# Moving half of a forward transform behind the transform of the convolution's kernel

## What is computed

```python
K = 2 * real(einsum('hn,hnl->hl', Ct, exp(dtA * l)))          # the convolution's kernel, per channel
Xf = rfft(x, n=2 * length); Kf = rfft(K, n=2 * length)
y = irfft(Xf * Kf)[:, :length]                                  # a long causal convolution
r = x + y + x * D
x = x0 + layernorm(r) * ln_w + ln_b                             # x is the normalised x0
```

## Time and profile before

| | |
|---|---|
| median of 3 runs | 901.05 us (900.11 to 901.35) |
| span of the profiled execution | 899.3 us |
| busy: TensorE matmul, weight load | 633.2 us (70%), 468.5 us (52%) |
| busy: VectorE | 635.0 us (71%) |
| busy: ScalarE | 445.1 us (49%) |
| busy: GpSimd | 456.7 us (51%) |
| mean granted clock of TensorE | 0.876 |

### The profile page before, as it was taken

How to read it: one execution, slowest core, us unless ns; L and a number is a source line. 1 busy time by engine, 2 the same in 40 slices (tenths; PEclk the granted TensorE clock), 3 DMA queues, 4 the chain that set the end, 5 groups by cost and what they waited for, 6 DMA issues and landing times. The chain is left out here.

```text
span 899.3 us, 21979 instructions
## 1 busy us (share of the span) xinstructions
PE 633.2 (70%) x7826; PEld 468.5 (52%) x7826; DVE 635.0 (71%) x1395; ACT 445.1 (49%) x873; POOL 456.7 (51%) x569
## 2 busy tenths in 40 slices
PE   0197973882059999324799998998963795999950
PEld 0073432562049999312566665665641564998850
DVE  6989988681048888387677777877741972888855
ACT  5632167670035555271766665665642242555534
POOL 1126767887637777510002222554573881677760
PEclk9978997896579999755899999999985997999985
DMA  9510001432134563242121322332111412454418
GB/s 287 132 37 1 0 0 45 83 80 58 44 60 90 102 93 84 85 162 60 45 83 50 91 73 73 78 105 74 49 36 37 80 34 48 84 97 93 93 27 281
DMA packets 131850, 70.51 MB, mean 78 GB/s; under 512 B 89535, under 2 KB 118725, under 8 KB 131746
## 3 DMA queue, kind: packets, MB, share of 16 engines
q1 hardware_dynamic: 121042, 50.46, 23.8%
q0 software_dynamic: 9088, 16.88, 6.9%
q10 hardware_dynamic: 1616, 1.77, 0.7%
HBM read 26.61 MB, written 30.50 MB: 64 GB/s over the span
## 5 line engine op out<-in xcount | busy, mean ns | idle before, releaser
L1437 ACT ACTIVATE ARENA<-banks,ARENA 128x256 f32<-128x256 f32 x312 | 122.2, 474 | 104.2 <-PE banks L1400 86.7
L2150 DVE TENSOR_REDUCE ARENA<-banks 128x4 f32<-128x1024 f32 (+1 forms) x128 | 122.7, 959 | 46.7 <-PE banks L1891 45.4
L1398 PE MATMUL banks<-ARENA,W1H 128*128 128x256 f16 x312 | 87.1, 279 | 65.3 <-DMA ARENA<-slots 58.2
L2072 ACT ACTIVATE ARENA<-banks 128x1536 f32<-128x1536 f32 x64 | 92.8, 1450 | 58.2 <-PE banks L1919 58.2
L1412 PE MATMUL banks<-W2L,ARENA 128*128 x624 | 110.8, 220 | 3.2 <-DVE ARENA L1450 2.4
L1414 PE MATMUL banks<-W2H,ARENA 128*128 x624 | 110.2, 219 | 0.0
L1413 PE MATMUL banks<-W2H,ARENA 128*128 x624 | 110.1, 219 | 0.0
L1388 POOL DMA_INDIRECT expert_out_g<-ARENA x78 | 80.6, 1034 | 47.7 <-issue 25.8
L1388 POOL DMA_INDIRECT expert_out_f<-ARENA x78 | 80.0, 1026 | 37.5 <-issue 25.8
L1471 DVE TENSOR_TENSOR ARENA<-ARENA 128x1024 f16<-128x1024 f32 x78 | 95.6, 1226 | 2.7
L1000 POOL DMA_INDIRECT slots<-ARENA,PLACE x64 | 77.6, 1212 | 28.4 <-issue 20.4
(11 more groups left out here) (312 smaller groups left out, 1812.0 us busy)
## 6 DMA issues: line engine op xcount, KB each, us to landing
spread<-ARENA SPq DMA_DIRECT2D x96, 64.0 KB, 2.1
ARENA<-expert_out_f SPq DMA_DIRECT2D x8, 512.0 KB, 7.4
ARENA<-spread SPq DMA_DIRECT2D x16, 256.0 KB, 3.0
ARENA<-spread SPq DMA_DIRECT2D x32, 128.0 KB, 3.0
ARENA<-expert_out_g SPq DMA_DIRECT2D x8, 512.0 KB, 7.3
XT<-in_w SPq DMA_DIRECT2D x10, 256.0 KB, 7.7
slots<-EMPTY SPq DMA_DIRECT2D x16, 129.0 KB, 4.5
ARENA<-in_w SPq DMA_DIRECT2D x8, 256.0 KB, 6.8
```

Source lines behind the costliest of these rows:

```text
L1398: pe.matmul(out, t.W1H[:, e, ms], XST[i][:, 0], start=True, stop=False)
L1437: ins = nc.scalar.activation(HF[i % 2][:, m], UP[i % 2][:, m], ACT.Gelu, bias=BIAS[i % 4][:, m:m + 1], scale=1.0 / WS)
L2072: nc.scalar.activation(PR[x % 2], t.psum_all[:, 5:8, :], ACT.Exp, scale=1.0 / LOGIT).then_inc(exps, 1)
L2150: dve.tensor_reduce(MX[:, G // 2, tile, :, :, G % 2].rearrange("p s a -> p a s"), src, AX.X, ALU.max).then_inc(m_red, 1)
```

## The change

In TensorE's list `forward(0, 1)` moves from behind `forward(0, 0)` to behind the last matmul of line 549. Nothing else is changed.

```diff
             pe.wait_ge(dct_in, 48)
             pe.wait_ge(xn_ready, 1)
             forward(0, 0)
-            forward(0, 1)
 
             pe.wait_ge(e2_ready, 1)
             pe.wait_ge(e1_ready, 1)
...
                     ins = pe.matmul(ps[4][:, D * ft:D * ft + D], FW[:, st, P * ft:P * ft + P], KLAG[:, st, :],
                                     start=(st == 0), stop=(st == TPB - 1))
             ins.then_inc(kf_mm, 1)
+            forward(0, 1)
             for g in range(1, NCG):
                 pe.wait_ge(xn_ready, g + 1)
                 for k in range(2):
```

## The result

| | before | after |
|---|---|---|
| median, measured together | 901.32 us (9 runs) | 899.03 us (897.44 to 900.7, 9 runs) |
| ratio | | 0.9974, 95% interval 0.9963 to 0.9985 |
| span of the profiled execution | 899.3 us | 897.2 us |
| mean granted clock | 0.876 | 0.876 |

The change makes the kernel 0.26% faster, 2.3 us, where 0.32% and 2.84 us were forecast. A second set of 7 runs of the same kernel on another occasion gave 0.9965 (0.9949 to 0.9981), 3.2 us; the two intervals overlap, and the forecast lies between the two values.

What follows compares the result with a forecast made beforehand. VectorE was taken as the bound from 62.64 on, with its wait for line 540's transposes ahead; 2.84 us gained at line 699 shifts everything behind: 901.05 - 2.84 = 898.2 us, range 895.4 to 901.5.

Steps and rivals of the forecast that it cites:

- What bounds the stage: First stage ends at GpSimd's first dispatch (137.16) plus a fixed train of 64; moving that dispatch moves the kernel's end equally.
- Where the first half ends, and the start of the small products: TensorE, group 0: first half ends at 46.56, small products start at 46.88 instead of 50.08, 3.20 us earlier.
- The new floor on VectorE: VectorE's memsets end at 59.65, then three semaphore additions; line 699 starts at 59.8, gain 2.84 us (2.65 to 2.95).
- ScalarE's cover: ScalarE's normalisation of group 1 and line 446's copy finish ahead of line 549, due at 61.86, with 0.7 us to spare.
- The moved half: Behind line 549 it starts at 65.64, ends at 70.9, before line 726 wants it at 71.62; cost nothing, up to 1.0.
- Rival A: TensorE stays at half clock through the moved half, VectorE waits 1.0 us; gain 1.8, 899.2 us; chance 0.12.
- The clock at the last inverse: Last inverse half, at 130.07, partly at half rate; its clock may fall better or worse, -1.8 to +1.5 us, taken at 0.
- Rival B: Full clock through group 1 removes VectorE's 0.5 wait, and last inverse half runs 1.8 us shorter; 895.9 us; chance 0.15.
- Rivals C and D: VectorE and GpSimd delay each other in the dispatch train: C loses the gain (901.2, chance 0.16), D is slower (904.2, 0.07).

Runs made afterwards that it cites:

- the one with only the second set of fillers: Changed kernel plus 3 matmuls with unused results, behind the last inverse's transposes (2 ahead of the gate, 1 behind it); 0.9957 of the kernel before.

## Why the prediction was right

The forecast of 898.2 us against 901.05 is 0.32%; measured were 0.26 and 0.35%. Its steps, one by one:

- *What bounds the stage.* Right. All 13 profiles, of both kernels and the 11 of the experiments, have the stage's end 111.3 to 114.0 us behind the first dispatch: 113.31 before, 113.32 after. That nothing behind the stage changes held only to about 2 us (648.8 to 651.0 us in the 13 profiles), whatever the edit.
- *Where the first half ends, and the start of the small products.* 46.88 forecast, 46.85 measured. The prediction took TensorE's return to the full rate at 45.3 as given. In other executions the start of the pair was slower or faster: the small products of the kernels with both halves ahead and no fillers at the start began at 49.26, 50.08 and 50.95, those with one half ahead at 46.84 to 47.31. So the gain at this point is 2 to 4 us from one execution to the next, and 3.2 was that of the one I read.
- *The new floor on VectorE.* Mis-sized by 0.33 us. I let the three additions to semaphores cost up to 0.30; line 699 started 0.02 behind the start of the memset ahead of it, at 59.47 for the 59.8 forecast. The gain at line 699 was 3.17 us, not 2.84; 0.13 of it is that this execution was that much earlier from the start.
- *ScalarE's cover.* 0.7 us forecast, 0.57 measured (its wait for line 543's result).
- *The moved half.* Right in the sum (no wait), too careful in the size: I expected the clock back by 69.3 and 0.7 us of cover; it was back within line 548, and the cover was 2.9. The times of the clock's changes did not stay put: the granted clock fell between 50 and 51 us here (0.84 in that microsecond, 0.50 in the next), where before it fell between 55 and 56, and it was back between 64 and 65. In the three kernels that have the change and fillers at the last inverse only, it came back later, within the half, which took 3.92 to 4.46 us and still ended 1.7 us or more before VectorE wanted it. Rival A does not hold here, and neither does the rule of the Trainium skill in "TensorE: Matmul & The Clock Gate", section "HAM oscillation — how this bites in real kernels", as I applied it to this place. One step earlier in the same list the half is slow: between small products and transposes it took 5.84 us. Behind the kernel's transform the clock was back, behind the small products it was not.
- *The clock at the last inverse.* This is the term that was furthest off in the profiles, though within its bounds. I took it at 0 within -1.8 and +1.5. In both profiles of the changed kernel it was +1.06 against that of the kernel before, at the first half of that inverse, where I had only looked at the second. The place is shown by the windows. That the change causes it is not: in the nine profiles without fillers ahead of it, that half took 3.71 us twice and 5.21 to 6.71 seven times, with and without the change, and the one profile of the kernel before is one of the two. The medians show no loss either: 3.2 us would be a ratio of 0.9965, which lies in both intervals.

- *Rival B* (the clock pays as well) came true in one part, without effect: VectorE's wait of 0.5 for the inverse is gone, although group 1 still took 8.65 us for 16 records (9.41 before, 7.03 for group 2); but VectorE's line 81 behind it is then held beside GpSimd's line 286 as before, and ends 3.22 us earlier, no more (first before, then after). With the fillers ahead of the second half of the last inverse the other part comes true too. 

```profile
92.35 2.38 DVE L81 TENSOR_TENSOR NRM<-STATS 128x8 f32<-128x8 f32 x1
```

```profile
89.13 2.38 DVE L81 TENSOR_TENSOR NRM<-STATS 128x8 f32<-128x8 f32 x1
```

- *Rivals C and D* (dispatches and VectorE holding each other up) moved the train by at most 2 us from the 113.31 of the kernel before, in any profile, and by 0.01 between the two kernels.

The path and the overlap were foreseen, and the gain at line 744, 3.21 us, is near the 2.84 of the forecast. That the first dispatch came close too (2.15) has a share of luck: two errors stood against each other, 0.33 too little at VectorE's floor, and 1.06 too much by a clock that might have fallen otherwise in either profile.

What stays open: why the rest of the program differed by 1.4 us between two profiles of the same kernel, which is over half the gain of 2.3; and how often the last inverse meets the half clock in the kernel before and in the changed one.

## What to carry to other kernels

Look at what the first dependent instruction of a serial chain is waiting for: if it is only the engine's order, put ahead of it just as much independent work as fits until its operand is there, and the rest behind the last step of the chain that another engine waits for, not one step before. Then look at how far it shifts the consumers on the other engines, for the floor is theirs. And where a long wait of TensorE stands ahead of work that is on the path, a few matmuls without use in that wait may pay for themselves; here the profiles show it for the path, and the medians only hint at it.

## What the hardware showed

- The granted clock of TensorE isn't a function of the instruction stream. Up to the last inverse, the changed kernel and the one with only the second set of fillers run the same matmuls; the first half of that inverse took 5.40 us in one and 3.71 in the other, behind 3.08 and 3.09 us of idleness. Group 0's pair, coming out of 40 us of idleness, took 8.62, 9.24 or 9.89 us in three kernels that are the same up to there. Of changes of a few microseconds, part is this draw.
- 2.74 us of matmuls without use in a wait of 3.1 us, and 3.04 us in two shorter ones, stood together in three profiles, and both halves ran at the full rate in all three. Over the 13 profiles the first half ran at the full rate in four of four with its fillers and in two of nine without, the second in four of four and in three of nine.
- Small fp32 products of 16 columns pass at the same rate at either clock (9.6 to 9.96 us for 256 records), while the 16 transposes took 1.17 us at a granted 1.00 (with the half ahead of them) and 1.89 at a granted 0.50. The clock fell while the small products ran without a gap (between 55 and 56 us before, between 50 and 51 after).
- Early in a profile the granted clock doesn't show the rate: it reads 1.00 from 42 to 45 us in the kernel before, where the records start 0.85 us apart, half the rate of those from 45.27 on; and 1.00 from 61 to 64 us in the kernel with both halves behind, where line 547 took 3.78 us, as line 549 did before at a granted 0.50. There the spacing of the records tells the rate.
- Three increments of semaphores by VectorE's own queue, between a memset and a waiting copy, were hidden completely: the copy started 0.02 us behind the start of the memset (59.47, 59.45).
